# Turning x and the context by 32 x 32 blocks on VectorE and a regroup in DRAM, in place of TensorE's transposes, in an attention kernel

## What is computed

```python
h = _ln(x, g1, be1)
x = _attn(h, h, Wq1, Wk1, Wv1, Wo1, bo1) + x
h = _ln(x, g2, be2)
x = _attn(h, context, Wq2, Wk2, Wv2, Wo2, bo2) + x
h = _ln(x, g3, be3)
y = h @ Wp + bp
a, gate = (y[..., :FF_HID], y[..., FF_HID:])
x = a * jax.nn.gelu(gate, approximate=False) @ W2 + b2 + x
```

## Time and profile before

| | |
|---|---|
| median of three runs | 3026.1 us |
| the profiled execution's own time | 3024.38 us |
| its span, first to last instruction | 3022.6 us |
| TensorE busy | 2958.4 us (98%) |
| VectorE busy | 2304.4 us (76%) |
| ScalarE busy | 1878.4 us (62%) |
| GpSimd busy | 1429.0 us (47%) |
| moved by DMA | 640.79 MB, mean 212 GB/s |
| mean granted TensorE clock | 0.995 of full speed |

### The profile page before, as it was taken

The page is one execution under the profiler, slowest core; times in us unless marked ns, Lnnn a source line. Parts: engine busy times, 40 slices in busy tenths (PEclk is TensorE's granted clock), DMA queues, the critical chain, the costliest instruction groups (busy, mean ns, idle before and its releaser), DMA issues. The chain is left out here.

```text
span 3022.6 us, 77287 instructions
## 1 busy us (share of the span) xinstructions
PE 2958.4 (98%) x25480; PEld 2579.0 (85%) x25480; DVE 2304.4 (76%) x3858; ACT 1878.4 (62%) x5618; POOL 1429.0 (47%) x976
## 2 busy tenths in 40 slices
PE   7999999999999999999999999999999979999999
PEld 6888888888888888788888888888888858888888
DVE  5877777777777777788888888888888856666664
ACT  6666666666666666677777777777777733232322
POOL 4555555555555555555555555555555531111110
PEclk9999999999999999999999999999999989999999
DMA  7787878788887887888888888888888841112211
GB/s 239 228 243 243 243 244 244 243 243 246 244 245 240 245 247 239 261 252 256 253 253 254 253 254 253 254 251 260 251 252 254 248 148 56 56 62 62 69 56 35
DMA packets 475243, 640.79 MB, mean 212 GB/s; under 512 B 58944, under 2 KB 405952, under 8 KB 474944
## 3 DMA queue, kind: packets, MB, share of 16 engines
q1 hardware_dynamic: 473824, 639.96, 69.8%
q10 hardware_dynamic: 1376, 0.27, 0.1%
HBM read 338.57 MB, written 301.47 MB: 212 GB/s over the span
## 5 line engine op out<-in xcount | busy, mean ns | idle before, releaser
L602 POOL TENSOR_TENSOR at_probs<-at_probs,at_row_inv 128x1024 f32<-128x1024 f32 x512 | 969.6, 1894 | 1059.5 <-DVE at_row_inv L808 1059.4
L653 ACT ACTIVATE at_probs<-at_ps_s,at_neg_max 128x256 f32<-128x256 f32 x2048 | 945.7, 473 | 143.2 <-DVE at_neg_max L781 94.7
L781 DVE TENSOR_REDUCE at_neg_max<-at_ps_s 128x2 f32<-128x512 f32 x1024 | 660.4, 684 | 194.7 <-PE at_ps_s L959 191.1
L800 DVE STREAM_TRANSPOSE at_blocks<-at_probs 128x1024 f32<-128x1024 f32 x512 | 630.8, 1232 | 2.1 <-POOL at_probs L602 2.0
L706 ACT ACTIVATE at_qk_hi<-at_ps_qk 128x512 fp32r<-128x512 f32 x512 | 305.7, 597 | 324.5 <-PE at_ps_s L959 183.4
L978 PE MATMUL at_ps_o<-at_probs_t,at_v 128*64 128x256 f32 x4096 | 500.9, 386 | 1.9 <-DMA at_probs_t<-at_turns 1.9
L891 PE MATMUL at_ps_qk<-at_h_hi,w_hi 128*128 128x256 f32 x1536 | 432.1, 304 | 12.7 <-ACT at_h_hi L676 6.2
L653 ACT ACTIVATION_READ_ACCUMULATOR at_probs<-at_ps_s,at_neg_max 128x1 f32 x2048 | 414.6, 202 | 0.0
L978 PEld LDWEIGHTS at_ps_o<-at_probs_t,at_v 128*64 128x64 f32 x4096 | 271.9, 137 | 148.6 <-issue 3.2
L891 PE MATMUL at_ps_qk<-at_h_hi,w_lo 128*128 128x256 f32 x1536 | 397.9, 281 | 0.0
L891 PEld LDWEIGHTS at_ps_qk<-at_h_hi,w_hi 128*128 128x128 f32 x1536 | 290.1, 189 | 125.3 <-issue 104.5
(11 more groups left out here) (107 smaller groups left out, 6598.6 us busy)
## 6 DMA issues: line engine op xcount, KB each, us to landing
at_turns<-at_blocks SPq DMA_DIRECT2D x2048, 128.0 KB, 2.5
at_probs_t<-at_turns SPq DMA_DIRECT2D x512, 512.0 KB, 4.4
at_xt<-in_x SPq DMA_DIRECT2D x32, 256.0 KB, 5.4
at_xres<-in_x SPq DMA_DIRECT2D x32, 256.0 KB, 3.2
after_self_attention<-at_yout SPq DMA_DIRECT2D x32, 256.0 KB, 2.6
at_xt<-after_self_attention SPq DMA_DIRECT2D x32, 256.0 KB, 5.4
at_xres<-after_self_attention SPq DMA_DIRECT2D x32, 256.0 KB, 3.7
after_cross_attention<-at_yout SPq DMA_DIRECT2D x32, 256.0 KB, 2.6
```

The source lines that it names most:

```text
L602: pool.tensor_tensor(tile, tile, scale, ALU.mult).then_inc(probs_ready, 1)
L653: last = act.activation(probs[:, slot % 2, h, t], scores[:, slot % 2, h, t], ACT.Exp, bias=neg_max[:, slot % 2, i:i + 1], accum_out=row_su ...
L781: nc.vector.tensor_reduce(neg_max[:, slot, r], scores[:, slot, h], AX_X, ALU.max, negate=True).then_inc(neg_max_ready, 1)
L800: nc.vector.transpose(blocks[:, slot].rearrange("p (j a q) -> p a j q", j=QUADS, q=QUAD), probs[:, slot].rearrange("p h t (k j q) -> p (h ...
```

## The change

- The normalised x of every sequence but the first, and each context, are turned as the probabilities are: VectorE turns the blocks (`turn_x`, `turn_context`, both L816 of the changed kernel), SyncE stores them by four DMAs (L536) to the DRAM tensors `x_turns` and `c_turns` and loads them back (`x_back`, L554; `c_t`, L550). TensorE transposes only the first x.
- x has one more link on its way and each one up to the turn is one double step sooner: statistics and normalisation in step 0, turn and store in step 2, load back in step 4, scale and shift at the end of step 4. The context is turned at the end of step 0, stored in step 2 and loaded back in step 4.
- On SyncE `load_next` stands ahead of the probability loads of step 0.
- The scale and shift reads `x_back` in SBUF in runs of 32 elements in place of PSUM; so do the three operations that split the context. The high part of the context is two activations, for 128 channels each.
- x is normalised in place, and the residual is added in place in `xres`, which is what is stored. The load of x waits for its turn. x and the context have block buffers of their own.
- The feed-forward part's first residual waits for all outputs of attention.

```diff
+        c_t = sb("c_t", [P, QUADS * X_TURN], F32)
...
+        x_back = sb("x_back", [P, QUADS * X_TURN], F32)
+        x_turns = nc.dram_tensor(tag + "x_turns", [QUADS, QUAD, QUADS, X_TURN], F32).ap()
...
+        def by_token(buffer):
+
+            return buffer.rearrange("p (i t k q) -> p k t i q", i=QUADS, t=TT, k=KT)
+
+        def tokens(rows):
+
+            return rows.rearrange("p (t i q) -> p t i q", t=TT, i=QUADS)
...
-                sp.wait_ge(xnorm_ready, b)
+                if isinstance(b, int) and b == 1:
+                    sp.wait_ge(h_transposed, 1)
+                else:
+                    sp.wait_ge(x_turned, b - 1)
                 sp.dma_start(xt[:], rows(x_in[stage][local])).then_inc(x_loaded, 16)
                 if stage == CROSS:
                     if counts(local):
-                        sp.wait_ge(c_transposed, local)
...
-                sp.dma_start(rows(x_out[stage][b - n * stage]), yout[:]).then_inc(y_stored, 16)
+                sp.dma_start(rows(x_out[stage][b - n * stage]), xres[:]).then_inc(y_stored, 16)
...
+            def store_bands(buffer, bands, stored):
+                for i in range(QUADS):
+                    sp.dma_start(bands[:, :, i].rearrange("j k n -> k j n"),
+                                 buffer[QUAD * i:QUAD * (i + 1)].rearrange("k (j n) -> k j n", j=QUADS)
+                                 ).then_inc(stored, 16)
+
+            def store_context(local):
+                sp.wait_ge(c_turned, local + 1)
+                store_bands(c_blocks, c_turns, c_turn_stored)
+
+            def store_x(b):
+                sp.wait_ge(x_turned, b)
+                store_bands(x_blocks, x_turns, x_turn_stored)
+
+            def load_context_back(local):
+                sp.wait_ge(c_turn_stored, 16 * QUADS * (local + 1))
+                sp.dma_start(c_t[:], c_turns.rearrange("j k i n -> (j k) (i n)")).then_inc(c_back_loaded, 16)
+
+            def load_x_back(b):
+                sp.wait_ge(x_turn_stored, 16 * QUADS * b)
+                sp.dma_start(x_back[:], x_turns.rearrange("j k i n -> (j k) (i n)")).then_inc(x_back_loaded, 16)
...
+                context = ahead(part, stage) and stage_ahead(part, stage) == CROSS
+                if ahead(part, stage) and p == 0:
+                    load_next(b + 1, stage_ahead(part, stage))
                 for pair in (p, p + 1):
                     if alive(part, pair, LOADED):
                         load_turn(b, pair)
-                if ahead(part, stage) and p == 0:
-                    load_next(b + 1, stage_ahead(part, stage))
+                if context and p == 2:
+                    store_context(b + 1 - n)
+                if ahead(part, stage) and p == 4:
+                    load_x_back(b + 1)
+                if context and p == 4:
+                    load_context_back(b + 1 - n)
                 for pair in (p, p + 1):
                     if alive(part, pair, TURNED):
                         store_turn(b, pair)
+                if ahead(part, stage) and p == 2:
+                    store_x(b + 1)
...
-                pool.tensor_tensor(xnorm[:], xt[:], mean, ALU.subtract).then_inc(centred, 1)
+                pool.tensor_tensor(xt[:], xt[:], mean, ALU.subtract).then_inc(centred, 1)
...
-                if ahead(part, stage) and p == 2:
+                if ahead(part, stage) and p == 0:
                     norm_power(b + 1)
                     norm_apply(b + 1)
...
+                first = isinstance(b, int) and b == 0
+                if first:
+                    act.wait_ge(h_transposed, 1)
+                else:
+                    act.wait_ge(x_back_loaded, 16 * b)
+                    act.wait_ge(h_ready, b)
                 for k in range(KT):
-                    last = act.activation(h_t[:, k], ps_misc[:, k * SEQ:(k + 1) * SEQ], ACT.Identity,
+                    out, source = ((h_t[:, k], ps_misc[:, k * SEQ:(k + 1) * SEQ]) if first else
+                                   (tokens(h_t[:, k]), by_token(x_back[:])[:, k]))
+                    last = act.activation(out, source, ACT.Identity,
...
-                act.wait_ge(c_t_ready, b - n + 1)
+                act.wait_ge(c_back_loaded, 16 * (b - n + 1))
...
-                act.activation(c_hi[:], c_t[:], ACT.Copy).then_inc(c_hi_ready, 1)
+                for k in range(KT):
+                    last = act.activation(tokens(c_hi[:, k]), by_token(c_t[:])[:, k], ACT.Copy)
+                last.then_inc(c_hi_ready, 1)
...
-                    if ahead(part, stage) and p == TURN_H:
-                        scale_shift(b + 1, stage_ahead(part, stage))
                     if ahead(part, stage) and p == 6:
...
+                if ahead(part, stage) and p == 4:
+                    scale_shift(b + 1, stage_ahead(part, stage))
...
+            def turn_rows(rows, blocks_of, turned_rows):
+                nc.vector.transpose(blocks_of[:].rearrange("p (j a q) -> p a j q", j=QUADS, q=QUAD),
+                                    rows.rearrange("p t (k j q) -> p (t k) j q", j=QUADS, q=QUAD)
+                                    ).then_inc(turned_rows, 1)
+
+            def turn_context(b):
+
+                local = b - n
+                dve.wait_ge(ctx_loaded, 32 * (local + 1))
+                if counts(local):
+                    dve.wait_ge(c_turn_stored, 16 * QUADS * local)
+                turn_rows(ct[:], c_blocks, c_turned)
+
+            def turn_x(b):
+
+                dve.wait_ge(xnorm_ready, b + 1)
+                if counts(c := 16 * QUADS * (b - 1)):
+                    dve.wait_ge(x_turn_stored, c)
+                turn_rows(xt[:], x_blocks, x_turned)
...
-                nc.vector.tensor_tensor(yout[:].rearrange("p t d -> p (t d)"), ps_y[:],
+                nc.vector.tensor_tensor(xres[:].rearrange("p t d -> p (t d)"), ps_y[:],
...
+                nc.vector.tensor_tensor(tokens(c_hi[64:P, 1]), by_token(c_t[64:P])[:, 1],
...
+                if ahead(part, stage) and p == 2:
+                    turn_x(b + 1)
                 if alive(part, p + 1, NORMED):
                     inverse(b, p + 1)
-                if ahead(part, stage) and p == 2:
+                if ahead(part, stage) and p == 0:
                     norm_stats(b + 1)
...
-                if ahead(part, stage) and p == TURN_CONTEXT and stage_ahead(part, stage) == CROSS:
-                    context_copy(b + 1 - n)
                 if alive(part, p, SCORES):
                     maxima(g - SCORES, (p - SCORES) % 2, 1)
...
+                if ahead(part, stage) and p == 0 and stage_ahead(part, stage) == CROSS:
+                    turn_context(b + 1)
...
-                if ahead(part, stage) and p == TURN_CONTEXT + 2 and stage_ahead(part, stage) == CROSS:
-                    pe.wait_ge(c_t_ready, b + 2 - n)
-                if ahead(part, stage) and p == TURN_H + 2:
-                    pe.wait_ge(h_t_ready, b + 2)
...
-            def transpose_h(b, stage):
-                pe.wait_ge(xnorm_ready, b + 1)
-                if counts(c := PAIRS // 2 * b - 1):
-                    pe.wait_ge(v_ready, c)
-                if stage == CROSS:
-                    pe.wait_ge(c_t_ready, b - n + 1)
-                transposes(xnorm, h_transposed)
-
-            def transpose_context(b):
-                pe.wait_ge(ctx_loaded, 32 * (b - n + 1))
-                pe.wait_ge(v_ready, PAIRS // 2 * b - 2)
-                transposes(ct, c_transposed)
...
-                if ahead(part, stage) and p == TURN_CONTEXT and stage_ahead(part, stage) == CROSS:
-                    transpose_context(b + 1)
-                if ahead(part, stage) and p == TURN_H:
-                    transpose_h(b + 1, stage_ahead(part, stage))
...
             pool.wait_ge(f.consts_loaded, 64)
+            pool.wait_ge(before, before_count)
             residual(0, 0)
```

44 lines of the change are left out of this document (22 added, 22 removed).

## The result

The changed kernel takes **3117.18 us** (median of 4 runs, 3109.09 to 3119.50), the kernel before 3025.58 beside it (4 runs). The ratio is 1.0298, interval 1.0282 to 1.0314: 3% slower, where 3008 and "faster" were predicted, outside the range.

A forecast was written before the change was run, and what follows sets the result against it. TensorE was taken to set the pace, with VectorE late in cross-attention's p = 0. Terms: 41.8 + 8.4 - 4.8 - 15.2 - 8.1 - 4 = 18.1 us less, so 3008 us as a median; range 2984 to 3026.

The forecast's parts named there:

- first sign of being wrong: On TensorE: the prediction is wrong if TensorE waits for at_probs_t, the reloaded probabilities.
- The removal, 0.44 us a group: On TensorE: 95 groups of four transposes go, 0.44 us each, 41.8 us, all on the path.
- Self p = 6, 0.15: Self-attention's last step: scale-and-shift ahead of o_hi moves the second projection to 4.44, 0.15 past 4.29; cost 4.8 us.
- Cross p = 6, 9.33: Cross-attention's last step: o_lo at 2.00 puts the second projection 0.49 us past 3.95; the step lasts 9.33; cost 15.2 us.
- Cross p = 4 recovers 0.27: Cross-attention's third step: without the context's copy on VectorE it falls to the bare 8.84; 31 x 0.27 = 8.4 us gained.
- The turned context costs p = 2 nothing: Cross-attention's second step: the context's turn pushes o_lo by at most 0.6 us; nothing to 0.2 a sequence, taken as 0.
- The context's two activations, 0.26 in p = 0: ScalarE, cross-attention: copying the context's high part in two activations delays p = 0 by 0.26 us a sequence, 8.1 us.
- The start, 4 us: At the start: x_back queues behind the cross weights and reaches ScalarE late; 4 us taken, bounds 0 and 6.
- SyncE's queue, charged nothing: Cross-attention: pair 4's probability load stands behind eight more stores, 2.8 us later, with 0.8 us of room left; no charge.
- The load of x goes ahead of the probability loads: SyncE's queue in step 0: named as an edit, with no cost given.
- the probability loads come late: Rival: pair 4's weighing in cross sequences stalls 1.2 us for a late load, 37 us in all, time 3045; chance 0.13.
- The bounds of its own case: Whole time: 2995 to 3018 us, with the pair of activations at 0.7 or 1.1 and the start at 0 or 6.

The follow-up runs named there:

- experiment 3: The changed kernel with the context transposed by TensorE and copied by VectorE in step 2 as before, x still turned: 3060.54 us, ratio 1.0113.
- first run of experiment 4: The changed kernel with scale-and-shift moved from the end of step 4 into step 6, ahead of h's high part: 3093.25 us, ratio 1.0222.
- all-turned version: The changed kernel with scale-and-shift in step 6, loads back last, cross weights early, only x ahead of step 0's reloads, context behind: 3008.14 us, ratio 0.9948.
- mended: Another name for the all-turned version, the changed kernel with four DMA and scale-and-shift placements altered: 3008.14 us, ratio 0.9948.
- experiment 4: The changed kernel with scale-and-shift in step 6: 3093.25 us; then also x_back and c_t loaded behind step 4's eight stores: 3051.40.
- experiment 2: The kernel before with eight spare stores in step 2 of cross sequences: 3031.00 us with 64 KB each, 3032.30 with 2 KB each.
- experiment 1: The kernel before with cross-attention's x and context loads ahead of step 0's reloads: 3057.08 us; the reverse, in the changed kernel: 3107.19.
- first kernel of experiment 1: The kernel before with only the loads of x and context put ahead of step 0's reloads in cross-attention: 3057.08 us, ratio 1.0103.

## Why the prediction was wrong

The prediction's own first sign of being wrong, TensorE waiting for at_probs_t, is what the trace shows. Its terms in turn:

- **The removal, 0.44 us a group: right.** Self sequences went from 37.64 to 37.20 wherever scale-and-shift was out of the way, and p = 4 from 9.74 to 9.30. The Trainium skill ("TensorE: Matmul & The Clock Gate", Part 4: PE-mode transpose) gives a transpose about 275 ns; taken as a cost, that would make a group 4 x 0.275 = 1.1 us, an estimate from that page, and the starts rule it out.
- **Self p = 6, 0.15: place right, size 0.30.** After, scale-and-shift takes 0.98 us from start to start (0.91 assumed), o_lo starts 2.05 us into the step and the second projection 4.52 (4.44 predicted). That is 0.23 past 4.29; the other 0.07 comes behind it and is not explained. ScalarE, VectorE and TensorE of one such step:

```profile
361.68 1.09 ACT L717 ACTIVATE at_h_t<-at_x_back,at_beta,at_gamma 128x256 f32<-128x256 f32 x2
362.66 0.58 ACT L754 ACTIVATE at_o_hi<-at_ps_o 128x512 fp32r<-128x512 f32 x1
```

```profile
363.28 0.69 DVE L884 TENSOR_TENSOR at_o_lo<-at_ps_o,at_o_hi 128x512 fp32r<-128x512 f32 x1 [1.27 <-ACT at_o_hi L754]
```

```profile
361.23 0.39 PE L964 MATMUL at_ps_qk<-at_h_hi,w_hi 128*128 128x256 f32 x1
...
365.75 0.38 PE L964 MATMUL at_ps_qk<-at_h_hi,w_hi 128*128 128x256 f32 x1
...
370.83 0.38 PE L964 MATMUL at_ps_qk<-at_h_hi,w_hi 128*128 128x256 f32 x1
```

- **Cross p = 6, 9.33: measured 9.42, by luck.** The predicted mechanism didn't act there. p = 4 ends so late, behind its wait for the reload, that scale-and-shift is mostly done by then, and o_lo starts 1.12 us into p = 6 on the mean, not 2.00. In the 22 of 29 sequences at full granted clock the second projection starts 3.93 to 4.10 us in, near the bare 3.95. In the other seven the clock fell behind p = 4's wait and the step lasted 9.56 to 10.42 us; that is 9.1 us over the 29, about 0.3 of the 0.58 above 8.84. Waits for the step's own reloads, in 9 of 29, add 0.15. One of the seven, TensorE, VectorE's o_lo, and the busy time of the step:

```profile
1919.17 1.08 PE L1037 MATMUL at_ps_o<-at_probs_t,at_v 128*64 128x256 f32 x8 [2.59 <-DMA at_probs_t<-at_turns]
1920.18 0.38 PE L964 MATMUL at_ps_qk<-at_h_hi,w_hi 128*128 128x256 f32 x1
...
1925.75 0.28 PE L964 MATMUL at_ps_qk<-at_h_hi,w_hi 128*128 128x256 f32 x1
```

```profile
1921.27 0.69 DVE L884 TENSOR_TENSOR at_o_lo<-at_ps_o,at_o_hi 128x512 fp32r<-128x512 f32 x1 [3.12 <-ACT at_o_hi L754]
```

```profile
1920.19:1930.61 10.42, 10.42 (x87) 9.34 (x85) 6.66 (x10) 6.94 (x22) 2.69 (x2) 0.84 0.68 214
```

  The mechanism does show where p = 4 is not late. With the context on TensorE (experiment 3) o_lo starts 2.04 us into p = 6, the second projection 4.51, and the step lasts 9.48. With scale-and-shift moved away (first run of experiment 4) p = 6 is still 9.35, with as much clock lost, and 8.91 once the loads back are last too.
- **Cross p = 4 recovers 0.27: hidden, then seen.** The second projection of p = 4 starts 3.95 us in after, 4.14 before, and the bare 8.84 appears in 9 of 29 sequences of the all-turned version, where the reload comes in time.
- **The turned context costs p = 2 nothing: right** (8.88 after, 8.84 mended).
- **The context's two activations, 0.26 in p = 0: wrong.** After, p = 0 falls to 9.33 and 9.39 in the sequences with timely reloads, below the 9.56 of before. The two take 0.61 us from start to start in the all-turned version, the one 0.52. at_c_hi holds p = 0 only when scale-and-shift stands in step 6 ahead of it (10.21), a case the prediction didn't have.
- **The start, 4 us: 12.** Mechanism right, x_back behind the weights; the landing was 14.1 us and ScalarE's wait 8.97, above the upper bound of 6 for the start.
- **SyncE's queue, charged nothing: this step failed**, at two places.

  *Step 4.* The room was worked out for the first of the step's two reloads, 0.8 us, and that was right: after, it lands 6.14 us into the step and is needed at 7.01. The second reload was not worked out. With eight stores ahead SyncE has no pause between the two, and it goes out 0.5 us behind the first instead of 1.3; with two loads behind it as well, it lands 9.52 us into the step, where a bare step needs it at 7.88. That is the wait of 1.56 us. The 1.02 of the loads back and the 0.88 that stays behind the eight stores are its two parts (experiment 4). Eight stores in the kernel before cost nothing (experiment 2), as TensorE came no sooner there.

  *Step 0.* "The load of x goes ahead of the probability loads" was named among the edits and given no price. It has one of 1.04 us x 31 = 32 us by itself (experiment 1). The trace of before had most of the numbers: the two reloads of p = 0 landed 4.79 and 6.21 us into the step and were needed at 7.68 and 8.60, 2.9 and 2.4 us of room. The order alone made them 3.35 and 3.2 us later. About 1.8 of the first one's delay is the issue of three DMAs ahead, and the rest lies under the 2 us of transfer of x and the context.
- **The rival "the probability loads come late"** named the mechanism. Its place was nearly right: the weighing of pair 4 is the first in its step and waits in 2 of 29 sequences, the one behind it in all. Its price of 1.2 us was counted from the bare 8.84; measured, p = 4 is 1.92 above that (1.21 above before). p = 0, which it didn't name, is 1.33 above before. With a chance of 0.13 it was far too low: it had two places in which to come true, and only one was weighed. The landings of p = 0 lengthened by 1.7 and 2.1 us, and by as much in experiment 1, which moves no more bytes than the kernel before. The Trainium skill ("DMA: Bandwidth & Descriptors", Latency and other measured facts) gives HBM's access as 0.2 us on average and 2 us at high load, a difference of 1.8, an estimate from that page and near this number. But the mean load was the same in experiment 1; what changed is which loads stand just ahead, and no run splits a landing into its parts.
- **The bounds of its own case** don't follow from its terms. The pair at 0.7 and the start at 0 would give 2993, the pair at 1.1 and the start at 6 3022, in place of 2995 and 3018. That plays no part in the miss.

## What to carry to other kernels

Where several engines' work hangs on one DMA queue, price a load that is moved ahead of an urgent one twice, by its issue and by its longer way to landing, and a load put directly behind it as well: neither was free here. Small stores ahead cost their issue, hardly their bytes. Where urgent loads come in pairs, work out the second too: a fuller queue pushes the two together, and it was the second that was late here. Taking work off the bounding engine pays only as far as what feeds it has room; work out that room at every step that is passed, not at the one that looks thinnest. When a mend moves no time, look at the step where another wait grew by the same amount.

## What the runs showed that was not expected

A stall of TensorE can cost more than itself. In one cross sequence of the changed kernel p = 0 waited 1.59 + 0.25 us for reloads and lasted 12.24, and p = 2, with no wait, 9.87 in place of 8.84. TensorE's rows, and the busy time of that p = 2:

```profile
1376.22 1.08 PE L1037 MATMUL at_ps_o<-at_probs_t,at_v 128*64 128x256 f32 x8 [1.59 <-DMA at_probs_t<-at_turns]
1377.55 1.64 PE L1037 MATMUL at_ps_o<-at_probs_t,at_v 128*64 128x256 f32 x8 [0.25 <-DMA at_probs_t<-at_turns]
```

```profile
1379.12:1388.99 9.87, 9.87 (x87) 8.79 (x85) 6.94 (x10) 5.70 (x19) 2.79 (x2) 0.89 0.88 253
```

The granted clock is 0.89 there: some of it ran at 1.2 GHz, and eight weighings took 1.64 us where they take 1.08. Between 1375 and 2325 nine stretches of 25 us show such a dip (0.93 mostly), together up to 14 us of the 78.9, 9 of them in p = 6; the kernel before and the mended one have none there. Nor have the cross sequences of the first kernel of experiment 1, with 28.2 us of waits for reloads, so which stalls cost clock stays open. In the start, where TensorE waited for x_back, the stretch from 50 to 75 us has 0.79, against 1.00 before.
